# Attention and experts of a layer in one block, with three signals between them, and the first loads of a layer ahead of the other start-up work

## What is computed

```python
# layer 0
h = layernorm(x) * (1 + ca) + sa
x = x + ga * attention0(h)            # 16 heads, bias -slope * |i - j|, out projection
h = layernorm(x) * (1 + cb) + sb
g = softmax(h @ Wr); top2_w, top2_idx = top_k(g, 2); top2_w /= sum(top2_w)
x = x + gb * sum(top2_w * (relu(h @ W1[e]) @ W2[e]))   # e in top2_idx
# layer 1
h = layernorm(x) * (1 + ca) + sa
x = x + ga * attention1(h)            # layer norm inside, 16 heads, + xn
h = layernorm(x) * (1 + cb) + sb
xn = rmsnorm(h) * rms_w; s = softmax(xn @ gate_w.T)
x = x + gb * max(s) * (silu(xn @ W1[e] + b1[e]) @ W2[e] + b2[e])   # e = argmax(s)
```

## Time and profile before

| | |
|---|---|
| median of three runs | 1952.15 us |
| the profiled execution | 1953.77 us |
| its span (first to last instruction) | 1951.8 us |
| TensorE busy | 1575.8 us (81%) |
| VectorE busy | 1459.5 us (75%) |
| ScalarE busy | 1127.4 us (58%) |
| GpSimd busy | 682.5 us (35%) |
| all DMA | 193.24 MB, mean 99 GB/s |

### The profile page before, as it was taken

One profiled execution on the slowest core, in us unless ns is written; L12 is line 12 of the kernel. 1 busy time (PEld: TensorE's weight loads), 2 busy tenths in 40 slices (PEclk: granted clock), 3 DMA queues, 4 the chain that ended last, 5 costly groups with the idle time before them and its releaser, 6 DMA issues. The chain is left out here.

```text
span 1951.8 us, 43561 instructions
## 1 busy us (share of the span) xinstructions
PE 1575.8 (81%) x14034; PEld 1147.8 (59%) x14034; DVE 1459.5 (75%) x4531; ACT 1127.4 (58%) x2182; POOL 682.5 (35%) x742
## 2 busy tenths in 40 slices
PE   3799999999989836999982787877887878836996
PEld 1466666666666625999981454554554545525885
DVE  4688888888888834777763888889899898833664
ACT  1477777777777621222222677777777777733443
POOL 3011232323233253555552222334334343232444
PEclk9899999999999967999995899999999999977998
DMA  3455555544445431222224555655656655453442
GB/s 92 62 79 84 93 100 89 98 89 83 81 78 85 64 92 53 75 70 75 70 65 97 111 114 108 149 119 126 146 118 140 121 111 121 78 187 103 129 129 74
DMA packets 271641, 193.24 MB, mean 99 GB/s; under 512 B 26559, under 2 KB 257889, under 8 KB 271156
## 3 DMA queue, kind: packets, MB, share of 16 engines
q1 hardware_dynamic: 256056, 155.43, 40.8%
q0 software_dynamic: 15360, 35.03, 5.8%
HBM read 95.36 MB, written 53.18 MB: 76 GB/s over the span
## 5 line engine op out<-in xcount | busy, mean ns | idle before, releaser
L944 DVE TENSOR_REDUCE mx<-A 128x2 f32<-128x512 f32 x1024 | 683.4, 680 | 145.1 <-PE A L1221 136.8
L774 ACT ACTIVATE probs<-B 128x1024 f32<-128x1024 f32 x512 | 522.0, 1020 | 218.1 <-PE B L1251 128.7
L1221 PE MATMUL A<-stack 126*128 126x256 bf16 x2048 | 391.3, 280 | 115.8 <-DVE mx L944 77.6
L1248 PE MATMUL B<-stack 128*128 128x256 bf16 x2048 | 355.9, 276 | 8.9 <-DMA stack<-mrow 7.6
L1221 PEld LDWEIGHTS A<-stack 126*128 126x128 bf16 x2048 | 159.8, 99 | 270.8 <-DVE mx L944 161.8
L1266 PE MATMUL M<-probs,vals 128*32 128x256 f32 x4096 | 282.0, 391 | 41.9 <-DVE On L967 37.2
L625 POOL TENSOR_TENSOR parts<-rem,parts 128x512 bf16<-128x512 f32 x64 | 73.9, 1155 | 540.4 <-ACT parts L753 450.8
L1248 PEld LDWEIGHTS B<-stack 128*128 128x128 bf16 x2048 | 202.0, 101 | 45.5 <-DMA stack<-mrow 11.5
L1647 PE MATMUL A<-shared 128*128 128x128 f32 x1792 | 219.5, 276 | 8.4 <-issue 8.4
L1647 PEld LDWEIGHTS A<-shared 128*128 128x128 f32 x1792 | 208.8, 192 | 12.7 <-issue 12.7
L1638 PE MATMUL B<-xtT,shared 128*128 128x256 f32 x896 | 205.7, 383 | 0.0
(11 more groups left out here) (198 smaller groups left out, 2359.8 us busy)
## 6 DMA issues: line engine op xcount, KB each, us to landing
stack<-parts SPq DMA_DIRECT2D x768, 64.0 KB
xt<-gathered SPq DMA_DIRECT2D x112, 132.0 KB
probs<-gathered SPq DMA_DIRECT2D x40, 256.0 KB
back_rows<-mod_rows SPq DMA_DIRECT2D x64, 128.0 KB, 4.0
x_mid<-X SPq DMA_DIRECT2D x64, 128.0 KB, 3.9
w<-in_w SPq DMA_DIRECT2D x32, 256.0 KB
yt<-expert_out SPq DMA_DIRECT2D x64, 128.0 KB
X<-in_x SPq DMA_DIRECT2D x32, 128.0 KB
```

Of the source, the lines that this page charges most:

```text
L774: act.activation(probs[c % 4][:, :, :, :], Bp[BUFFER[c]][:, :, :, :], ACT.Exp, scale=EXP_SCALE[l][c // 4]).then_inc(b_exp.handle, 1)
L944: dve.tensor_reduce(mx[u][:, h, :], A[h % 2][:, :, :], AX.X, ALU.max).then_inc(a_max.handle, 1)
L1221: ins = pe.matmul(A[h % 2][:, t, :], stack[u][0:n, h, 0, t * P:(t + 1) * P], stack[u][0:n, h, 1, :], start=True, stop=True)
L1248: ins = pe.matmul(Bp[BUFFER[c]][:, j, t, :], stack[u][:, h, 1, t * P:(t + 1) * P], stack[u][:, h, 0, :], start=True, stop=(l == 1))
```

## The change

Each layer's attention and experts now stand in one block inside one `cleanup_on_exit`, and the block is asked for without GpSimd's drain at its end. `attention` returns three semaphores. GpSimd increments `all_scattered` after the waits for its row scatters, VectorE increments `tables_ready` after its tables, SyncE increments `all_loaded` after the waits for its transfers. In the experts part SyncE, VectorE, ScalarE and TensorE wait for all three (`begin`) before their first work. What they did ahead of it stays ahead: their start values, and ScalarE's table load. GpSimd does not wait for them; its first work there waits for a result. The engines' lists of work are otherwise the same, and each still branches from its attention code to its experts code.

At the start of attention SyncE gives 6 increments (x_in, front_in, x2_out), then issues `load_front` of tile 0, and only then gives the other 24 and, in layer 1, issues the two fills. Without the lines that are only indented otherwise, the diff is:

```diff
         for layer in range(2):
             with nc.cleanup_on_exit():
-                attention(nc, layer, locals())
-            with nc.cleanup_on_exit():
-                experts(nc, layer, locals())
+                with nc.Block(no_gpsimd_drain=True) as block:
+                    handed = attention(nc, layer, block, locals())
+                    experts(nc, layer, block, handed, locals())
...
-def attention(nc, l, g):
+def attention(nc, l, block, g):
...
     run_ready, padded = sem("run_ready"), sem("slack_padded")
+    all_scattered, tables_ready, all_loaded = sem("all_scattered"), sem("tables_ready"), sem("all_loaded")
...
-    with nc.Block() as block:
-
         @block.sync
         def _(sp):
...
             if l == 1:
                 weights += [(b1[:, :, :], a["b1"]), (b2[:, :, :], a["b2"].broadcast_to([P, E, D]))]
+        more_weights = iter(weights)
+        for t in (x_in, front_in, x2_out):
+            t.start(sp)
 
+        def start_others():
+            for t in (stack_in, m_in, x1_out, back_in, x2_in, ga_in, gate_in):
+                t.start(sp)
+            if l:
                 for u in range(2):
                     sp.dma_start(stack[u][BROW:BROW + 2 * NB, :, 0, :], a["no_rows"].bitcast(BF16)).then_inc(lin_in, 16)
-            more_weights = iter(weights)
-            for t in (x_in, stack_in, m_in, x1_out, front_in, back_in, x2_out, x2_in, ga_in, gate_in):
-                t.start(sp)
 
             def tick(at):
...
                 if at(3) and l == 0:
                     load_front(*at(3))
+            if at(3) and at(3)[0] == 0:
+                start_others()
                 if at(1):
                     stack_up(*at(1), 0)
...
             for u in range(2):
                 sp.wait_ge(*((x2_in[u], x2_in.of(B // 2 - 1)) if l else (x1_out[u], x1_out.of(B // 2 - 1))))
+        sp.sem_inc(all_loaded, 1)
 
         @block.gpsimd
...
             for v in range(HELD):
                 pool.wait_ge(scat_out[v], scat_out.of(B // HELD - 1))
+        pool.sem_inc(all_scattered, 1)
...
             ch.link(dve.tensor_scalar(tile_e[:, 0:slots], tab[:, 0, :], float(E - 1), None, ALU.min))
             ch.settle()
+        dve.sem_inc(tables_ready, 1)
...
             run_ticks(tick)
+    return all_scattered, tables_ready, all_loaded
 
 
-def experts(nc, l, g):
+def experts(nc, l, block, handed, g):
...
+    all_scattered, tables_ready, all_loaded = handed
+
+    def begin(eng):
+
+        eng.wait_ge(all_scattered, 1)
+        eng.wait_ge(tables_ready, 1)
+        eng.wait_ge(all_loaded, 1)
...
+        begin(sp)
             for n in range(2):
                 load_tile(*tile(0, n))
...
+        begin(dve)
             for n in range(2):
                 e = stage_w1(*tile(0, n))
...
+        begin(act)
             if l:
                 for n in range(2):
                     read_xT(*tile(0, n))
...
+        begin(pe)
             for n in range(2):
                 turn_x(*tile(0, n))
```

More of the change, by code:

```diff
@@ L1401, in experts, with tick @@
-def experts(nc, l, g):
+        def tick(at):
+            if l and at(3):
+                load_front(*at(3))
+            if at(0):
+                stack_up(*at(0), 1)
+            if at(-1):
+                stack_max(*at(-1), 1)
+            if l and at(2):
+                store_x2(*at(2))
+                load_ga(*at(2))
+            if at(-1):
+                load_back(*at(-1))
+            if at(3) and l == 0:
+                load_front(*at(3))
+            if at(3) and at(3)[0] == 0:
+                start_others()
+            if at(1):
+                stack_up(*at(1), 0)
+            if at(-2):
+                if l:
+                    load_gate(*held(at, -2))
+                else:
+                    store_x1(*at(-2))
+            if l and at(1):
+                load_x2(*at(1))
+            if at(0):
+                stack_max(*at(0), 0)
+            if at(-2):
+                for dst, src in itertools.islice(more_weights, 1):
+                    sp.dma_start(dst, src).then_inc(weights_in, 16)
@@ new lines, in _, with load_tile, load_extra @@
+    @block.sync
+    def _(sp):
+        xt_in.start(sp)
+        extra_in.start(sp)
+        def load_tile(s, k, u):
+            row = sp.value_load(tile_row[0:1, bass.ds(s, 1)], min_val=0, max_val=E * REGION + (TAIL - 1) * TOK)
+            sp.wait_ge(xt_T.handle, xt_T.after(s - 2))
+            sp.wait_ge(end_read.handle, end_read.after(s - 2))
+            sp.dma_start(xt[u][:, :, :], gathered[l][bass.ds(row, TOK), 0:W].rearrange("(t p) d -> p t d", p=P))\
+                .then_inc(xt_in[u], 16)
+        def load_extra(s, k, u):
+            row = sp.value_load(tile_row[0:1, bass.ds(s, 1)], min_val=0, max_val=E * REGION + (TAIL - 1) * TOK)
+            sp.wait_ge(y_done.handle, y_done.after(s - 2))
+            sp.dma_start(extra[u], gathered[l][bass.ds(row, TOK), BASE:WX].rearrange("(t p) d -> p t d", p=P))\
+                .then_inc(extra_in[u], 16)
+        begin(sp)
+        for n in range(2):
+            load_tile(*tile(0, n))
+        for k in range(pairs - 1):
+            for n in range(2):
+                load_tile(*tile(k, n + 2))
+                if l:
+                    load_extra(*tile(k, n))
+        if l:
+            for n in range(2):
+                load_extra(*tile(pairs - 1, n))
@@ new lines, in _, with scatter @@
+    @block.gpsimd
+    def _(pool):
+        ch = Chain(pool, pool_order)
+        def scatter(s, k, u):
+            pool.wait_ge(y_done.handle, y_done.after(s))
+            ch.apart()
+            for t in range(NT):
+                dest = bass.IndirectOffsetOnAxis(ap=row_dest[s % OUT][:, t:t + 1], axis=0)
+                if l:
+                    ins = pool.indirect_dma_start(expert_out[l], dest, yt[:, s % OUT, t, :], None,
+                                                  bounds_check=B * S - 1, oob_is_err=False)
+                else:
+                    ins = pool.indirect_dma_start(expert_out[l], dest, yt[:, s % OUT, t, :], None)
+                ins.then_inc(yt_out[s % OUT], 16)
+        for k in range(pairs):
+            for n in range(2):
+                scatter(*tile(k, n))
+        for s in range(slots - OUT, slots):
+            pool.wait_ge(yt_out[s % OUT], yt_out.of(s // OUT))
```

1822 lines of the change are left out of this document (875 added, 947 removed).

## The result

| | before | after |
|---|---|---|
| median of the runs, us | 1950.68 (1947.67 to 1957.67, 4 runs) | 1926.01 (1924.71 to 1932.92, 4 runs) |
| ratio | 1 | 0.987, 95% interval 0.984 to 0.990 |
| profiled execution, us | 1953.77, span 1951.8 | 1932.92, span 1931.1 |

The change makes the kernel 24.7 us faster by the medians. The profiled execution of after is the slowest of its four runs, so its span is only 20.7 us shorter. I take 22 to 25 us as what there is to explain.

The account below looks back on a forecast made before the run. Tile pipelines bound the long stretches, GpSimd's drains the waits at the joins; 4.8 + 6.8 + 1.4 + 2.3 - 1.1 = 14.2 us off the median 1952.15 gives 1938.0 us, own range 1934 to 1942, full range 1926 to 1944.

Parts of the forecast that it names:

- The joins: Between attention and experts: without drain, barriers and clear, SyncE reads its first row 4.8 us (layer 0) and 6.8 us (layer 1) earlier.
- the branch: Join by branches: a fetch stall, warned of by the skill, would shrink layer 1's gain once over 1.2 us; none booked.
- part 2: End of a layer: GpSimd's drain moves to the clear's own drain, booked at zero; larger clears cost 1.1 us.
- the larger clears: Layer ends: one clear of 113 or 122 semaphores takes 0.65 or 0.69 us, +1.1 us in all.
- Rival (a): Layer ends: the drain goes altogether, 3.0 and 6.6 us more gained, 1928.4 us; chance 0.14.
- Rival (b): Layer ends: drains settle what has gathered, so the joins' 3.3 and 5.3 us are paid there, 1946.6 us; chance 0.09.
- The starts: First loads of a layer: issued ahead of most increments and the fills, layer 0 gains 1.4 us, layer 1 2.3 us.
- the landing: Layer 1's start: with no fills ahead in the DMA queues, the first loads land 0.6 us faster after issue.
- Rival (c): First tiles: the earlier starts' 3.7 us are lost because fills or second tile's loads are late, 1941.7 us; chance 0.07.
- Rival (d): TensorE's clock: the lower clock reaches more tiles, slower than before, 1968.9 us with seven more tiles; chance 0.04.

Follow-up runs that it names:

- Runs 5 and 6: Changed kernel plus a GpSimd drain at the joins, right behind its signal (5): 1928.32 us, ratio 0.987; ahead of the signal (6): 1936.83 us, ratio 0.992.
- run 8: Changed kernel plus a GpSimd drain right behind each attention batch's scatters and two in a row at the layers' ends: one execution of 2028.35 us.
- run 1: Changed kernel with GpSimd's plain drain put back at each layer's block exit: 1940.55 us, ratio 0.993 to the kernel before.
- Run 4: Changed kernel with SyncE's start-up order as in the kernel before (all semaphores and two fills first): 1934.37 us against 1954.18, ratio 0.990.
- run 3: Kernel before with only the change's start-up order of SyncE: 1949.91 us, ratio 0.998.
- the control: Changed kernel as it is, run again beside a candidate with early loads: 1929.26 us, ratio 0.989 to the kernel before.
- run 2: Kernel before with only GpSimd's drain left out at the end of all four blocks: 1935.02 us against 1953.66, ratio 0.990.
- run 12: Changed kernel plus late GpSimd drains behind 128 writes of layer 0's attention, 136 of its experts and 136 in layer 1: one execution of 1934.59 us.

## Why the prediction was right and wrong, step by step

**The joins were right.** 4.8 and 6.8 us were forecast for SyncE's first read. Measured from GpSimd's last wait to the first tile load it is 4.9 (5.8 to 0.85) and 6.9 (7.8 to 0.9). GpSimd's signal is the last of the three, as argued; the branch had no price. Runs 5 and 6 show the split: 8.6 us for the drains, some 3 for barriers and clears.

**The layers' ends were wrong, and this is nearly the whole of the error.** The step that failed is the one in part 2, "I therefore book the drain as moved, at zero". The term measures 9.3 to 9.6 us: from GpSimd's branch to SyncE's passing took 3.8 us before and takes 1.5 now; at the program's end 7.5 and 1.6. That is 8.2 us gained with the larger clears (0.65 and 0.69 us, 1.1 us more as forecast) already paid, so 9.3 for the drains; their own lengths add up to 9.6. Rival (a), the drain gone altogether, had its price (1928.4) and a chance of 0.14, and its outcome is what happened: 14.2 + 9.6 = 23.8 us against the 24.7 and 21.8 measured.

Two arguments led there. The first took over a rule: the drain waits for something on GpSimd, so "the next drain in line will meet that". The rule of the Trainium skill's "PSUM — Partial Sum Buffer", section "Engine vs sequencer instructions", that a drain waits until its engine is fully idle, agrees with run 8 in so far as a drain that begins while GpSimd is at work on writes outlasts that work. It does not cover the four drains of the kernel before, whose writes had landed and which still took 3.0 to 6.6 us, nor the 40 to 229 ns of the drains that came next in the changed kernel.

The second set aside accumulation because 144 writes cost 3.00 us, 80 cost 6.58 and 64 cost 5.28. The last two lie on a line through the origin, 82 ns for each write, and the line is the law. Layer 0's two points fall off it because most of their writes had been settled before. A price that does not rise in the order of the counts I read as one that does not depend on them. Rival (b), the joins' share paid at the ends, was also nearer to the mechanism than its refutation: with the exit's drain kept (run 1), layer 1's end does grow, from 6.58 to 7.73 us, though not by the 5.3 of the rival and not in layer 0. It needed a drain at the end to be charged, and there was none.

**The starts were nearly right.** Forecast 1.4 and 2.3. In layer 0 VectorE starts 1.5 us earlier. In layer 1 it is 1.7 for the issue, as forecast (1.6 us behind the barrier, held by VectorE's increments), but 0.25 and not 0.6 for the landing: from the last load's issue to GpSimd's start 3.05 us, where it was 3.3. Run 4, with the fills ahead again, has 3.71, so the fills ahead cost the landing 0.3 to 0.7 us, and the rest of it was no queue behind them. TensorE's first transpose is 1.8 us nearer to the barrier than in the kernel before, and 2.3 nearer than in run 4. Runs 3 and 4 put the order's worth at 3.8 us and at 1.4 to 5.5.

**The rest.** The ledger by places is 4.9 + 6.9 for the joins, 8.2 for the ends, 1.5 + 1.8 for the starts: 23.3 us. The profiled span shows 20.7; the other 2.6 were lost inside the long stretches of that execution, and single executions of the changed kernel differ by 12 us (1924 to 1936). Rival (c), the earlier starts lost again, is refuted by the times of run 3 alone. The traces cannot do it: from its start to GpSimd's signal, layer 0's attention is 1.1 of the 1.5 us shorter, and layer 1's, from barrier to signal, 0.5 of the 1.8 (731.7 before, 731.2 after); that stretch took 728.9 in the control and 733.6 in run 4, so single executions scatter by more than the gain. Rival (d) did not come as a loss: the mean granted clock of the changed kernel's profiled execution is 0.940 against 0.947, and 0.945 in the control's, with no new slow stretch in the slices behind the first two:

```profile
PE   2799999999999946999992787787888788855997
...
PEclk7799999999999967999995899999999999977999
```

The clock's row differs from the earlier trace rows in the first two slices, 7 and 7 for 9 and 8, which cover the setup and the first tiles of attention, and in the last. Two stretches of each kernel, the kernel before and then the changed one (start and end, length, then busy us and number of instructions of TensorE, its weight loads, VectorE, ScalarE and GpSimd, the granted clock, the DMA share and GB/s):

```profile
15.00:50.00 35.00, 8.43 (x23) 4.45 (x22) 13.06 (x65) 6.40 (x14) 1.15 (x1) 1.00 0.31 62
50.00:75.00 25.00, 14.57 (x69) 7.83 (x70) 16.28 (x35) 5.60 (x14) 1.15 (x1) 0.76 0.46 53
```

```profile
15.00:50.00 35.00, 6.00 (x22) 3.17 (x21) 13.15 (x65) 6.39 (x14) 1.15 (x1) 0.59 0.33 65
50.00:75.00 25.00, 17.45 (x86) 9.57 (x86) 17.28 (x38) 7.35 (x17) 1.15 (x1) 0.61 0.42 54
```

The clock was lower in this execution of the changed kernel, 0.59 against 1.00 up to 50 us and 0.61 against 0.76 behind it: a lower clock, as in rival (d), in this one place. It does not come from the start-up order: run 2, which has the old order, shows it too (0.59 and 0.69), and the changed kernel with other drains in run 12 does not (1.00 and 0.73). Yet TensorE did more by 75 us, 22 + 86 instructions against 23 + 69. So the earlier start was not given back here.

## What to carry to other kernels

A drain on GpSimd behind indirect writes is worth asking about wherever a block ends: if the writes are waited for by their semaphores, leaving the drain out of the block's exit saved 18.6 us here by itself, against 1.5 us for each barrier and clear taken away. Before a cost is booked as moved, ask what would charge it at the new place; and before a count is ruled out as its cause, divide each duration by its count, since two of four points on one line say more than the order of all four. Gains of a microsecond at a layer's start are better read from the place, measured from the last barrier, than from the total.

## What the runs showed of the hardware that was not expected

- GpSimd's drain costs 40 ns and 82 ns more for each indirect write issued since the last one, even if all have landed: 0.21 us behind 2, 8.54 us behind 104. Behind 120 and more a large part was already settled without a drain (1.02 us behind 120, 3.33 behind 128); behind 112 and fewer nothing was.
- It also waits for what is still under way: 7.0 us in the median of 64 drains issued right behind 2 or 4 writes, which ended 1.5 to 8.0 us after GpSimd had worked off the last of them.
- The debt is dropped in the cleanup between the layers, where the drains take 40 to 229 ns, with or without a drain before them.
